# Thirteen pieces for each block of attention's tail, and an earlier place for edge features and the carried row

## The chip, the cores and the metric

The kernel runs on one core of one Trainium2 chip. The metric is device time in microseconds (us). TensorE (PE) multiplies, VectorE (DVE) and ScalarE (ACT) work element by element and read PE's results from PSUM, GpSimd (POOL) issues the gathers and SyncE (SP) issues the other DMAs. Each engine runs its own instructions in order and waits on semaphores, so a wait holds back everything written behind it on that engine.

## The reference

A graph network of 2500 nodes (width 256) and 40000 edges sorted by destination, in four layers. The change is in the code for the last two:

```python
xn = _layernorm(x, ln1_g, ln1_b)
q, k, v = heads(xn @ Wq + bq), heads(xn @ Wk + bk), heads(xn @ Wv + bv)   # 8 heads of 32
ep = ef @ We + be                                  # edge features, 64 -> 32
scores = einsum('ehd,ehd->eh', q[dst], k[src] + ep[:, None, :]) * scale * ew[:, None]
attn = softmax of scores over the edges of one dst # segment_max, exp, segment_sum
x = x + alpha * (segment_sum(attn * v[src], dst) @ Wo + bo)
x = x + beta * (gelu(layernorm(x) @ W1 + b1) @ W2 + b2)
# and then, with t = layernorm(x): top 2 of 8 experts
gate = top2(softmax(t @ router.T)); out = t
for e in range(8):
    out = out + gate[:, e] * (gelu(t @ w1[e] + b1[e]) @ w2[e] + b2[e])
```

(The projections q, k, v are made in an earlier stage, `stage_sums_experts`, and `heads` and `top2` stand for a few lines each.)

## The kernel before

`stage_attention` does all of the above except the projections. It has two kinds of work, woven into one order by `order1`.

**Edge work** runs over 79 groups of 512 edges. Group i has a slot i, with a first half (`slotA`) and a second (`slotB`). There are 86 slots, since the sums of a group come `LAG` = 7 slots after its scores. In slot i DVE adds the features to the gathered keys (`add`, L1816), multiplies by the queries in PSUM (`multiply`, L1821), reduces to scores (`reduce`, L1827) and weighs the values of group i-6 (`weigh`, L1903). PE makes the queries (`queries`, psQ, one buffer, so it waits for `product` of the group before) and features (`features`, psE) of group i+1 in `slotB`, and the sums of group i-7 (`sums`, psG) in `slotA`. ACT copies features to SBUF (`att_epb`), scales the scores and copies the sums to `part`. Every fourth slot a softmax step turns the scores (S), maxima (M) and R on PE between DVE's scans; and every fourth group a carried row goes from `part` through PE (L2209), DVE (`carry`, att_crow) and back into PE's sums (L2173).

**Block work** runs over ten blocks of 256 nodes: normalise (`att`), turn, project (`wo`), normalise, turn (`turnN`), eight feed-forward pieces (`f` up, `y` down), normalise (`norm`), turn (`turnX`), router `logits`, gates and bias (`mix`), eight experts (`A` up, `C` down), `out`. `SEGMENTS` cuts it into pieces, one for each slot. Block b starts in slot 8b+17, so below "slot 0" to "slot 7" are the eight slots from a block's start to that of the next; piece 8 of a block shares a slot with piece 0 of the next. A piece lies between the two halves of its slot on every engine. `warm` issues twelve products with zeros (L2222) ahead of the three turns. Three PSUM banks (psR) are dealt out in turn; `y` holds bank 2 while `f` uses 0 and 1.

**SP** issues per slot: the store of `part`, the load of the windows three groups ahead and the load of group i+2 (ohT, qw, eft: `load_group`, two buffers, `in_got`). In a block's slot -1, which is slot 7 of the block before, it first issues the block's three loads (L2347 to L2349) and waits until they have landed (L2375, `load`), before it goes on with the slot.

## Time and profile before

| | us |
|---|---|
| median of 3 runs (lowest, highest) | 1970.42 (1964.58, 1979.68) |
| the profiled execution, its own time | 1965.13 |
| its span, first to last instruction | 1963.7 |
| PE busy in the span | 1643.5 (84%) |
| DVE, POOL, ACT busy | 969.5, 794.7, 581.4 |
| share of full TensorE clock, mean | 0.906 |

Attention's stage begins at 949.6 us with POOL's first gather. Slots 0 to 16 have no block work; from slot 17 to the last edge slot both kinds run together; the last two blocks end alone. To read the rows: a timeline row is a start, a duration, the engine, the line, the operation, its tiles and how many instructions it merges; in square brackets stands how long the engine sat idle before it and what released it. Matmuls overlap, so their rows do too. Numbers of tiles are left out (att_t is t1 or t3, att_h is h or h1, g_mw either expert weight, g_f either feed-forward weight).

### The profile page before, as it was taken

The page shows a single profiled execution, that of the slowest core. Times are in us where ns is not written, and L with a number is a line of the kernel's source. Part 1 is how long each engine was busy: PE and PEld are TensorE (multiplying, and loading weights), DVE is VectorE, ACT ScalarE, POOL GpSimd, SP SyncE. Part 2 cuts the span into 40 slices and gives each one's busy share as a digit, 9 for nine tenths or more (in the row PEclk, how much of TensorE's full clock was granted, in tenths as well). Part 3 has the DMA queues.
Part 4 walks back from the last instruction along what each step waited for, and adds up shares of the span by engine and source line. Part 5 has one row for each costly group of instructions (what it writes and reads, how often), then busy time and mean ns, then how long its engine had stood idle before and what let it go on. Part 6 is the DMA issues. An engine that isn't in the chain of part 4 may idle for free.

```text
span 1963.7 us, 22797 instructions
## 1 busy us (share of the span) xinstructions
PE 1643.5 (84%) x6693; PEld 1054.4 (54%) x6693; DVE 969.5 (49%) x2256; ACT 581.4 (30%) x1373; POOL 794.7 (40%) x769
## 2 busy tenths in 40 slices
PE   5899579669799899996357889989998999899786
PEld 2455125235445455565233566767666767666575
DVE  5522242123332534344477677777667676674222
ACT  2111002122131222322122344343434444343322
POOL 1000564766766665000567545444445444430000
PEclk9899669779899899998566999999999999999898
DMA  7246453644645645111679755545545555531000
GB/s 241 118 166 222 138 145 81 174 135 133 179 139 144 191 129 171 31 60 59 196 219 280 209 147 148 148 138 149 159 142 150 143 160 147 150 92 34 19 6 8
DMA packets 191807, 270.02 MB, mean 138 GB/s; under 512 B 28564, under 2 KB 156273, under 8 KB 189105
## 3 DMA queue, kind: packets, MB, share of 16 engines
q1 hardware_dynamic: 147665, 144.74, 23.6%
q0 software_dynamic: 44000, 123.64, 22.7%
q8 instruction: 58, 0.95, 0.2%
q14 instruction: 84, 0.69, 0.1%
HBM read 196.22 MB, written 72.06 MB: 137 GB/s over the span
## 4 chain that ended last, share of the span: by engine, by line
PE 34%; DVE 7%; issue 4%; ACT 3%; POOL 1%; DMA 1%; SPq 1%; POOLq 0%; DVEq 0%
PE att_psR L2289 8%; PE att_psR L2316 7%; PE att_psG L2174 5%; PE att_psR L2264 4%; PE att_psR L2273 4%; POOL att_kv L1796 1%; PE att_psQ L2150 1%; PE att_psR L2250 1%; PE att_psE L2157 1%; DVE att_stat L1938 1%; PE att_psR L2308 1%; PE att_psR L2222 1%; PE att_psR L2227 1%; DVE att_n L1949 1%; PE att_psG L2173 1%
## 5 line engine op out<-in xcount | busy, mean ns | idle before, releaser
L1796 POOL DMA_INDIRECT att_kv<-table_kv,g_srcI x314 | 360.2, 1147 | 515.8 <-PE att_psG L2174 276.2
L1107 POOL DMA_INDIRECT ex_hg<-table_h,z_idx x314 | 311.3, 991 | 182.7 <-issue 86.5
L1405 PE MATMUL ex_psG<-ex_hg,ex_oh 128*42 128x256 f32 x628 | 175.6, 420 | 51.9 <-DVE ex_oh L1121 31.9
L2289 PE MATMUL att_psR<-att_t,g_mw 128*128 128x256 f32 (+1 forms) x640 | 178.1, 428 | 18.6 <-ACT att_t L2128 18.6
L2174 PE MATMUL att_psG<-att_kv,att_oh 128*42 128x264 f32 x628 | 172.3, 416 | 1.6 <-DVE att_kv L1903 0.9
L2289 PEld LDWEIGHTS att_psR<-att_t,g_mw 128*128 128x128 f32 x640 | 132.5, 215 | 46.4 <-issue 28.1
L1816 DVE TENSOR_TENSOR att_kv<-att_kv,att_epb 128x1024 f32<-128x1024 f32 x79 | 96.5, 1221 | 119.6 <-ACT att_epb L2085 82.3
L1405 PEld LDWEIGHTS ex_psG<-ex_hg,ex_oh 128*42 128x42 f32 x628 | 70.4, 126 | 155.4 <-issue 69.8
L722 PE MATMUL tab_psH<-e_u,tab_xT 128*128 128x512 f32 x320 | 146.9, 611 | 5.3 <-DVE e_u L524 5.3
L2316 PE MATMUL att_psR<-g_mw,att_h 128*128 128x256 f32 x640 | 149.2, 381 | 0.0
L2316 PEld LDWEIGHTS att_psR<-g_mw,att_h 128*128 128x128 f32 x640 | 121.8, 192 | 19.7 <-issue 3.3
L1322 ACT ACTIVATE ex_h<-ex_psH,g_cols 128x512 f32<-128x512 f32 (+2 forms) x144 | 86.0, 605 | 145.1 <-PE ex_psH L1420 123.8
L2029 DVE SCALAR_TENSOR_TENSOR att_acc<-att_psR,att_gate,att_acc 128x256 f32<-128x256 f32 x160 | 70.0, 479 | 107.2 <-PE att_psR L2316 93.3
L1433 PE MATMUL ex_psC<-e_experts,ex_h 128*128 128x256 f32 x480 | 119.2, 402 | 3.8 <-DVE ex_acc L1251 3.8
L2133 ACT ACTIVATE att_h<-att_psR,g_cols 128x256 f32<-128x256 f32 (+1 forms) x160 | 66.2, 465 | 174.6 <-PE att_psR L2289 157.2
L1420 PE MATMUL ex_psH<-ex_h,e_experts 128*128 128x512 f32 (+2 forms) x288 | 112.3, 533 | 3.3 <-ACT ex_h L1322 3.2
L2174 PEld LDWEIGHTS att_psG<-att_kv,att_oh 128*42 128x42 f32 x628 | 70.3, 125 | 82.7 <-issue 39.0
L2150 PE MATMUL att_psQ<-att_qw,att_ohT 126*128 126x256 bf16 x316 | 53.7, 297 | 70.1 <-DMA att_eft<-in_eft 33.8
L1420 PE MATMUL ex_psH<-ex_xT,e_experts 128*128 128x512 f32 (+2 forms) x288 | 111.4, 532 | 0.0
L1433 PEld LDWEIGHTS ex_psC<-e_experts,ex_h 128*128 128x128 f32 x480 | 95.0, 202 | 26.1 <-issue 12.9
L1251 DVE SCALAR_TENSOR_TENSOR ex_acc<-ex_psC,ex_gate,ex_acc 128x256 f32<-128x256 f32 x120 | 51.8, 478 | 113.1 <-PE ex_psC L1433 110.4
L722 PEld LDWEIGHTS tab_psH<-e_u,tab_xT 128*128 128x128 f32 x320 | 61.6, 195 | 78.3 <-issue 70.8
(308 smaller groups left out, 2454.4 us busy)
## 6 DMA issues: line engine op xcount, KB each, us to landing
table_h<-tab_hs SPq DMA_DIRECT2D x20, 1024.0 KB, 3.9
att_eft<-in_eft SPq DMA_DIRECT2D x158, 64.0 KB
ex_db<-table_dst SPq DMA_DIRECT2D x79, 126.0 KB
table_ohT<-ex_ohT SPq DMA_DIRECT2D x79, 126.0 KB
att_ohT<-table_ohT SPq DMA_DIRECT2D x79, 126.0 KB
table_oh<-ex_oh SPq DMA_DIRECT2D x79, 84.0 KB
att_oh<-table_oh SPq DMA_DIRECT2D x79, 84.0 KB
ex_hg<-table_h,z_idx POOLq DMA_INDIRECT x314
```

The source lines that it names most:

```text
L722: ins = nc.tensor.matmul(psH[:, c % 4, :], xT[:, b % 2, k, q * P:(q + 1) * P], Wr[:, k, j * 512:(j + 1) * 512], start=(k == 0), stop=(k == ...
L1107: nc.gpsimd.indirect_dma_start(hg[:, t % RING0, :], None, d.h[:, :], bass.IndirectOffsetOnAxis(ap=g.idx0[:, t:t + 1], axis=0)).then_inc(go ...
L1322: nc.scalar.activation((h1 if what == "A" else h2)[:, e % 2, o, 0:used(b)], psH[:, n % 3, 0:used(b)], ACT.Relu, bias=vec(g, "eb1" if what ...
L1405: ins = nc.tensor.matmul(psG[0:WG, 0:D], oh[:, i % 3, t % TP, :], hg[:, t % RING0, :], start=(t % TP == 0), stop=last)
L1420: ins = nc.tensor.matmul(psH[:, n % 3, 0:w_], w[:, e, k, o * P:(o + 1) * P], x[:, k, 0:w_], start=(k == 0), stop=(k == DK - 1))
L1433: ins = nc.tensor.matmul(psC[:, q, :], h2[:, e % 2, k, q * P:(q + 1) * P], g.w3[:, e, k, :], start=(k == 0), stop=(k == DK - 1))
L1796: nc.gpsimd.indirect_dma_start(kv[:, t % (RINGC * TP), H:H + 2 * D], None, d.kv[:, :], bass.IndirectOffsetOnAxis(ap=g.srcI[:, t:t + 1], ax ...
L1816: nc.vector.tensor_tensor(k, k, epb[:, i % 2, :, :].unsqueeze(2).to_broadcast([P, TP, H, DH]), ALU.add).then_inc(s.added, 1)
L2174: ins = nc.tensor.matmul(out[0:WG, :], oh[:, i % 3, t % TP, :], kv[:, t % (RINGC * TP), 0:H * VW], start=(t % TP == 0), stop=end)
L2264: ins = nc.tensor.matmul(out[:, 0:used(b)], g.f1[:, k, e * P:(e + 1) * P], t1[:, k, 0:used(b)], start=(k == 0), stop=(k == DK - 1))
L2289: ins = nc.tensor.matmul(out[:, c * CB:c * CB + used(b)], g.mw1[:, e, k, c * P:(c + 1) * P], t3[:, k, 0:used(b)], start=(k == 0), stop=(k ...
L2316: ins = nc.tensor.matmul(out[:, q * D:(q + 1) * D], h1[:, n % 3, k, q * P:(q + 1) * P], g.mw2[:, e, k, :], start=(k == 0), stop=(k == DK - 1))
```

## The change

The blocks are cut into thirteen pieces in place of ten, and the starts stay 8 slots apart, except that the last block may start two slots sooner (slot 87, `SLOTS + 1`). So pieces 8 to 12 of a block share slots with pieces 0 to 4 of the next. The first normalising (`att`) on DVE and the turn behind it (`turnA`) on PE are now one slot apart, `turnN` and `turnX` have slots of their own, and `logits` comes ahead of expert 0. The first turn and `turnN` lose their zero products; the output projection and `mix` get them. The features of group i+1 move from the second half of slot i to the first, behind the sums, on PE and on ACT. The turn of S comes behind the sums, the carried row ahead of the queries. The wait for the loads of a group moves from `queries` to `features`, and SP's wait for its buffer from `ep_made` to `q_ready`. The banks 0, 1, 2 are dealt out in turn, but 0 and 1 alone from a block's first `f` to its `norm`.

```diff
 SEGMENTS = (
     (("att", 0),),
+    (("turnA", 0),),
     (("wo", 0),),
-    (("turnN", 0), ("f", 0), ("f", 1), ("y", 0), ("f", 2), ("y", 1)),
-    (("f", 3), ("y", 2), ("f", 4), ("y", 3), ("f", 5), ("y", 4)),
-    (("f", 6), ("y", 5), ("f", 7), ("y", 6), ("y", 7), ("norm", 0)),
-    (("turnX", 0), ("A", 0), ("logits", 0), ("A", 1)),
-    (("mix", 0), ("A", 2), ("C", 0), ("A", 3)),
-    (("C", 1), ("A", 4), ("C", 2)),
-    (("A", 5), ("C", 3), ("A", 6), ("C", 4)),
+    (("turnN", 0),),
+    (("f", 0), ("f", 1), ("y", 0), ("f", 2), ("y", 1), ("f", 3), ("y", 2)),
+    (("f", 4), ("y", 3), ("f", 5), ("y", 4), ("f", 6), ("y", 5)),
+    (("f", 7), ("y", 6), ("y", 7), ("norm", 0)),
+    (("turnX", 0),),
+    (("logits", 0), ("A", 0), ("A", 1), ("A", 2)),
+    (("mix", 0), ("C", 0), ("A", 3), ("C", 1)),
+    (("A", 4), ("C", 2), ("A", 5)),
+    (("C", 3), ("A", 6), ("C", 4)),
     (("A", 7), ("C", 5), ("C", 6), ("C", 7), ("out", 0)))
...
-    start = [(NG // NC + 1) * (b + 1) + LAG + 2 if slots else 8 * b + 1 for b in range(NC)]
+    start = [min((NG // NC + 1) * (b + 1) + LAG + 2, SLOTS + 1) if slots else 8 * b + 1 for b in range(NC)]
...
-                elif unit == "f":
-                    n = e % 2
+                elif opened:
+                    n = turn_of = (turn_of + 1) % 3 if turn_of == 2 else (turn_of + 1) % 2
                 else:
-                    n, turn_of = turn_of, (turn_of + 1) % 3
+                    n = turn_of = (turn_of + 1) % 3
...
                         nc.scalar.copy(part[:, j % 3, :], psG[0:WG, 0:H * VW]).then_inc(s.part_ready, 1)
+                    if i + 1 < NG:
+                        features(i + 1)
...
                 def queries(i):
-                    pe.wait_ge(in_got[i % INS], 64 * (i // INS + 1))
...
                 def features(i):
+                    pe.wait_ge(in_got[i % INS], 64 * (i // INS + 1))
...
                 def slot_first(i):
                     j = i - LAG
+                    if 0 <= j < NG:
+                        sums(j)
+                    if i + 1 < NG:
+                        features(i + 1)
                     if (n := softmax(i, 0)) is not None:
...
                 def slot_second(i):
+                    j = i - LAG + 1
+                    if 0 < j < NG and j % SGG == 0:
+                        n = j // SGG
+                        pe.wait_ge(s.part_ready, j)
+                        pe.wait_ge(s.d_ready, n + 1)
+                        nc.tensor.matmul(psCarry, g.follow[0:WG, j - 1:j], part[:, (j - 1) % 3, :], start=True, stop=True).then_inc(s.carried, 1)
                     if i + 1 < NG:
                         queries(i + 1)
-                        features(i + 1)
...
                     if i >= INS:
-                        sp.wait_ge(s.ep_made, i - INS + 1)
+                        sp.wait_ge(s.q_ready, i - INS + 1)
```

How this moves instructions is seen best on PE. First the stretch behind a block's last `y` (L2273) before the change: queries, features, a turn of R, the sums, the zero products, the turn of the normalised block, then at once an expert's matmul (L2289), logits (L2296) and another expert's.

```order
L2273 MATMUL att_psR<-g_f,att_h 128x256 x4
L2150 MATMUL att_psQ<-att_qw,att_ohT 128x256 x4
L2157 MATMUL att_psE<-g_we,att_eft 128x64 x2
L2203 MATMUL att_psT<-g_ident,att_R 128x128
L2174 MATMUL att_psG<-att_kv,att_oh 42x264 x4
L2222 MATMUL att_psR<-g_none,g_identb 128x256 x12
L2227 MATMUL att_psR<-g_ident,att_n 128x128 x4
L2289 MATMUL att_psR<-att_t,g_mw 128x256 x4
L2296 MATMUL att_psR<-g_rt,att_t 128x8 x4
L2289 MATMUL att_psR<-att_t,g_mw 128x256 x4
```

The same place in the changed kernel, from the sums of slot 7 on (lines 4 to 6 higher; L2162 features, L2194 the turn of S, L2233 the turn, L2154 queries, L2300 logits):

```order
L2179 MATMUL att_psG<-att_kv,att_oh 42x264 x4
L2162 MATMUL att_psE<-g_we,att_eft 128x64 x2
L2194 MATMUL att_psT<-g_ident,att_S 128x128
L2228 MATMUL att_psR<-g_none,g_identb 128x256 x12
L2233 MATMUL att_psR<-g_ident,att_n 128x128 x4
L2154 MATMUL att_psQ<-att_qw,att_ohT 128x256 x4
L2211 MATMUL att_psT<-g_ident,att_M 1x128
L2212 MATMUL att_psT<-g_ident,att_M 1x128
L2179 MATMUL att_psG<-att_kv,att_oh 42x264 x4
L2162 MATMUL att_psE<-g_we,att_eft 128x64 x2
L2197 MATMUL att_psT<-g_ident,att_fnew 128x1
L2198 MATMUL att_psT<-g_ident,att_lnew 128x1
```

Logits and three experts' matmuls come only behind the last of these rows: the queries, two sums and two sets of features now stand between the turn's neighbours with no expert's matmul between them. The second place is the carried row (L2209) before the change, between the output projection (L2250) and `turnN`:

```order
L2250 MATMUL att_psR<-g_wo,att_t 128x256 x4
L2150 MATMUL att_psQ<-att_qw,att_ohT 128x256 x4
L2157 MATMUL att_psE<-g_we,att_eft 128x64 x2
L2209 MATMUL att_psT<-att_part,g_follow 1x264
L2174 MATMUL att_psG<-att_kv,att_oh 42x264 x3
L2173 MATMUL att_psG<-att_crow,g_ident 1x264
L2174 MATMUL att_psG<-att_kv,att_oh 42x264
L2222 MATMUL att_psR<-g_none,g_identb 128x256 x12
L2227 MATMUL att_psR<-g_ident,att_n 128x128 x4
```

And in the changed kernel (L2206 and L2178 are the carried row out and in, L2321 `C`, L2292 `A`, L2256 the output projection):

```order
L2233 MATMUL att_psR<-g_ident,att_n 128x128 x4
L2206 MATMUL att_psT<-att_part,g_follow 1x264
L2154 MATMUL att_psQ<-att_qw,att_ohT 128x256 x4
L2179 MATMUL att_psG<-att_kv,att_oh 42x264 x3
L2178 MATMUL att_psG<-att_crow,g_ident 1x264
L2179 MATMUL att_psG<-att_kv,att_oh 42x264
L2162 MATMUL att_psE<-g_we,att_eft 128x64 x2
L2292 MATMUL att_psR<-att_t,g_mw 128x256 x4
L2321 MATMUL att_psR<-g_mw,att_h 128x256 x4
L2292 MATMUL att_psR<-att_t,g_mw 128x256 x4
L2228 MATMUL att_psR<-g_none,g_identb 128x256 x12
L2256 MATMUL att_psR<-g_wo,att_t 128x256 x4
```

The queries now lie between the carried row's two products, the features behind both, and the turn, the projection and the next turn are each a slot apart with expert matmuls of the block before between them.

## Rows read from the trace of the kernel before

**Rows 1.** The page: TensorE's busy time, and its granted clock in 40 slices.
```profile
PE 1643.5 (84%) x6693; PEld 1054.4 (54%) x6693; DVE 969.5 (49%) x2256; ACT 581.4 (30%) x1373; POOL 794.7 (40%) x769
...
PEclk9899669779899899998566999999999999999898
```

**Rows 2.** The windows: stretch, its us, busy us (count) by engine, PEclk, DMA, GB/s.
```profile
1217.00:1307.00 90.00, 83.62 (x418) 62.17 (x417) 63.56 (x126) 38.00 (x101) 42.80 (x39) 0.96 0.52 150
...
1840.00:1910.00 70.00, 57.74 (x265) 47.87 (x264) 19.68 (x65) 21.15 (x38) 0.00 (x0) 0.88 0.05 16
```

**Rows 3.** The chain that ended last: each block's last `y`, blocks 0, 7, 9.
```profile
1124.40 1.74 PE att_psR L2273 x8
...
1756.37 1.74 PE att_psR L2273 x8
...
1908.13 1.74 PE att_psR L2273 x8
```

**Rows 4.** The waits, 1180 to 1720 us, PE's: total us, times, longest.
```profile
PE att_psR L2289 <- ACT att_t L2128: 12.8, 6, 2.1
...
PE att_psG L2173 <- DVE att_crow L1896: 10.1, 9, 1.6
...
PE att_psR L2264 <- ACT att_t L2118: 7.2, 6, 1.2
...
PE att_psT L2185 <- ACT att_S L2092: 5.1, 6, 0.9
...
PE att_psR L2227 <- DVE att_n L1961: 4.5, 6, 0.8
...
PE att_psR L2308 <- ACT att_gateT L2140: 3.3, 6, 0.5
```

**Rows 5.** The timeline of PE behind a block's last `y`.
```profile
1487.00 1.98 PE L2174 MATMUL att_psG<-att_kv,att_oh 128*42 128x264 f32 x8
1488.91 1.48 PE L2222 MATMUL att_psR<-g_none,g_identb 128*128 128x256 bf16 x12
...
1492.97 3.59 PE L2289 MATMUL att_psR<-att_t,g_mw 128*128 128x256 f32 x8 [2.14 <-ACT att_t L2128]
```

**Rows 6.** The timeline of SP: a store, a block's loads, the next group's load.
```profile
1505.41 0.37 SPq L2382 DMA_DIRECT2D table_o<-att_part  x1
...
1510.96 0.48 SPq L2349 DMA_DIRECT2D att_u<-table_u  x1
1518.34 0.29 SPq L2384 DMA_DIRECT2D table_o<-att_part  x1
...
1520.50 0.35 SPq L2327 DMA_DIRECT2D att_ohT<-table_ohT  x1
```

**Rows 7.** The waits of SP, 1180 to 1720 us: for the blocks' loads.
```profile
SPq L2375 <- DMA att_u<-table_u: 34.7, 6, 6.6
```

**Rows 8.** The timeline of PE, slots 17 to 19, hardly any block work.
```profile
1076.94 3.53 PE L2174 MATMUL att_psG<-att_kv,att_oh 128*42 128x264 f32 x8
...
1089.64 1.04 PE L2150 MATMUL att_psQ<-att_qw,att_ohT 126*128 126x256 bf16 x4 [3.72 <-DMA att_eft<-in_eft]
...
1099.14 1.53 PE L2174 MATMUL att_psG<-att_kv,att_oh 128*42 128x264 f32 x6
```

**Rows 9.** The timeline of SP there: the load of that group.
```profile
1085.75 0.36 SPq L2327 DMA_DIRECT2D att_ohT<-table_ohT  x1
```

**Rows 10.** The timeline of DVE behind the last `y`: `finish`, then the slot.
```profile
1486.16 0.75 DVE L1983 SCALAR_TENSOR_TENSOR att_u<-att_psR,g_rows,att_u 128x512 f32<-128x512 f32 x1
...
1490.06 1.23 DVE L1816 TENSOR_TENSOR att_kv<-att_kv,att_epb 128x1024 f32<-128x1024 f32 x1
...
1493.78 1.22 DVE L1903 TENSOR_TENSOR att_kv<-att_kv,att_p 128x1024 f32<-128x1024 f32 x1
```

**Rows 11.** The timeline of PE at the end: waits with no edge work left.
```profile
1843.87 0.66 PE L2227 MATMUL att_psR<-g_ident,att_n 128*128 128x128 f32 x4 [2.70 <-DVE att_n L1949]
...
1923.59 0.59 PE L2303 MATMUL att_psR<-g_ident,att_gate 128*8 128x128 f32 x2 [4.51 <-DVE att_gate L936]
```

More of the change, by code:

```diff
@@ L395 @@
 NCH = NREL * D // 512
+FIRST_LATER = 10
 WARM = 12
-FIRST_LATER = 10
 TABLES_FROM = NG // NB + 2
@@ L1737, in stage_attention @@
         assert redo or all(e > DONE_AFTER[b] for what, b, e in order if what == "load")
-        bank, before, last, turn_of = {}, {}, {}, 0
+        bank, before, last, turn_of, opened = {}, {}, {}, 0, False
         for what, b, e in order:
-            for unit in {"att": ("turnA",), "wo": ("wo",), "turnN": ("turnN",), "f": ("f",), "turnX": ("turnX",), "A": ("A",),
+            for unit in {"turnA": ("turnA",), "wo": ("wo",), "turnN": ("turnN",), "f": ("f",), "turnX": ("turnX",), "A": ("A",),
                          "logits": ("logits",), "mix": ("gateT", "bias"), "C": ("C",), "y": ("y",) if e == 0 else ()}.get(what, ()):
+                opened = opened or unit == "f"
                 if unit == "y":
                     n = 2
-                elif unit == "f":
-                    n = e % 2
+                elif opened:
+                    n = turn_of = (turn_of + 1) % 3 if turn_of == 2 else (turn_of + 1) % 2
                 else:
-                    n, turn_of = turn_of, (turn_of + 1) % 3
+                    n = turn_of = (turn_of + 1) % 3
                 bank[unit, b, e] = n
@@ L1752, in stage_attention @@
                 last[n] = (unit, b, e)
+            opened = opened and what != "norm"
         def drained(unit, b, e):
@@ L2107, in program @@
                                 scale(b)
-                            if b + 1 < NG:
-                                features(b + 1)
-                        if what == "att":
+                        if what == "turnA":
                             act.wait_ge(s.att_turned, b + 1)
@@ L2203, in slot_second @@
                         nc.tensor.transpose(psT[:, 0:P], R[:, :], g.ident[:, :]).then_inc(s.r_turned, 1)
-                    j = i - LAG + 1
-                    if 0 < j < NG and j % SGG == 0:
-                        n = j // SGG
-                        pe.wait_ge(s.part_ready, j)
-                        pe.wait_ge(s.d_ready, n + 1)
-                        nc.tensor.matmul(psCarry, g.follow[0:WG, j - 1:j], part[:, (j - 1) % 3, :], start=True, stop=True).then_inc(s.carried, 1)
                 def take(unit, b, e):
@@ L2232, in program @@
                         pe.wait_ge(g.loaded1, 16 * N_LOADED1)
+                        features(0)
                         queries(0)
-                        features(0)
                     for what, b, e in order:
@@ L2239, in program @@
                             slot_second(b)
-                        if what == "att":
+                        if what == "turnA":
                             out = take("turnA", b, e)
-                            warm(out)
                             pe.wait_ge(s.att_ready, b + 1)
@@ L2246, in program @@
                             out = take("wo", b, e)
+                            warm(out)
                             pe.wait_ge(s.aT_ready, b + 1)
@@ L2253, in program @@
                             out = take("turnN", b, e)
-                            warm(out)
                             pe.wait_ge(s.xn_ready, b + 1)
@@ L2300, in program @@
                             out = take("gateT", b, e)
+                            warm(out)
                             pe.wait_ge(s.gate_ready, b + 1)
```

5 lines of the change are left out of this document (1 added, 4 removed).

## The prediction, made before the changed kernel ran

> **What bounds the kernel now.** I read the page first: PE is busy for 84% of the span, and in the half that holds attention its slices show the full clock less a tenth [rows 1]. Then the windows: in 90 us of the steady part PE is busy 83.6 us, DVE 63.6, POOL 42.8, at a granted clock of 0.96 [rows 2]. Then the chain that ended last, for the pace: the last `y` of block 0 ends at 1126.1 us (1124.40 + 1.74), that of block 7 at 1758.1, that of block 9 at 1909.9 [rows 3]. So a period of eight slots takes (1758.1 - 1126.1) / 7 = 90.3 us, and 205.6 us follow from there to the end of the span. Then the waits: over six periods PE waited 43.0 us in the six rows shown, 7.2 a period, each of them short and at a fixed place: for the copy of the turned block ahead of the first expert (2.1) and ahead of the first `f` (1.2), for the carried row (1.7 in two waits), for the scores' turn (0.85), for the first turn's input (0.75) and for the gates' copy (0.55) [rows 4]. The clock costs (1 - 0.96) x 90 = 3.6 us more [rows 2]: after a wait of 2.14 us eight expert matmuls took 3.59 us where the same eight take 1.9 [rows 5]. So a period is some 79.5 us of PE's work, 7.2 of waits and 3.6 of clock. The steady part is bound by PE in order, and anything that fills its waits counts in full.
>
> **The change part by part.** No product is added or taken away on PE: three times twelve zero products before and after (1.3 us each, from 1488.91 to the turn). What moves is where PE waits.
>
> *Waits that go.* The carried row goes out ahead of the queries (0.45 us), which shortens its two waits, and expert matmuls of the block before stand between DVE's work and it: I take its 1.7 us as gone; the lower end is 2 x 0.45 = 0.9. `turnN` and the first `f` are a slot apart: 1.2 gone. First turn a slot behind `att`: 0.75 gone. The copy of the turned block ahead of the experts: 2.1 gone, since sums lie between. One of the two half-clock stretches, that behind the gates, loses the waits ahead of it: 1.8 gone. The gates' copy (0.55) stays. The scores' turn keeps its 0.85: it moves behind the sums, but in slot 3 ACT reaches the scaling only after the square root of the normalising that the projection at the end of slot 2 starts. Sum: 1.7 + 1.2 + 0.75 + 2.1 + 1.8 = 7.6 us a period.
>
> *A wait that comes.* Slots 6 and 7 are now light: PE has 2.6 us of block work (`f` 7, `y` 6, `y` 7) in one and 1.8 (zeros, turn) in the other, where it had 5 to 7. And the features of a group now come in the first half of the slot and carry the wait for the group's load, so they ask for it a whole piece of block work sooner. Take the end of the sums in slot 6 as zero. SP issues the store of that part 0.6 us later, and the last of the next block's loads 6.0 after that (1505.41 to 1511.44); it then waits 34.7 / 6 = 5.8 for their landing [rows 6, 7]; the next group's load is issued 3.3 later (1517.2 to 1520.50) [rows 6]; and from the first issue to the matmul that waits for it 3.9 us pass (1085.75 to 1089.64) [rows 8, 9]. Sum 19.6 us until the features of slot 0 can run. PE's own work up to there is: features 0.4, block 2.6, queries 0.45, sums 1.9, features 0.4, turn of S 0.2, zeros 1.3, turn 0.5, queries 0.45, turns of M 0.2, sums 1.9: 10.3 us. So PE stands still for 9.3 us in each period, where before 8 us of expert matmuls and more lay in between. Behind the waiting features stand logits and three experts, that is, everything. The same is seen in the trace where a block's load meets slots without block work: PE's sums of slot 17 start at 1076.94, and its queries wait for the load until 1089.64 [rows 8]. DVE sets a lower bound to the stall should the load be early: it holds the normalising for 3.9 us (1486.16 to 1490.06) and then four slot operations and two scans for 5.8, before it has weighed what the sums of slot 0 need [rows 10]; from the last `y` that is 9.8 us, of which PE can fill 5.4 with the work listed, so at least some 4 us of idle time stay.
>
> The net of a period is +9.3 - 7.6 = +1.7 us, over seven periods +12.
>
> *The start.* Block 0's last `y` comes in slot 23 instead of 21. Slots with little block work take 8 us (the sums of slot 17 start at 1076.94 and those of slot 19 at 1099.14, a block's load among them) [rows 8]. Work through slots 19 to 23 with the same 7.2 us from part to load, 3.6 for the normalising in slot 19 and the feed-forward pieces (13.8 us) in slots 21 to 23 gives the last `y` at some 1139 us, against 1126: +13. Slots 0 to 16 stay as they are: gathers and loads bound them; I take 0, with ends of -4 and +5.
>
> *The end.* After the last `y` of block 7 the new order has two edge slots less (5.2 us of sums and their kin, the counterpart of the +13), and in the last period queries and features run out sooner (1.7). Blocks 8 and 9 now overlap in seven pieces, not two. Of PE's waits between 1758 and 1910 us, 18.6 us, I expect 6.3 to stay: the two behind a last `y` (2.7 each) [rows 11] and short ones; 12.3 gone. The clock in 1840 to 1910 is 0.88 [rows 2], 8.4 us lost; half of the end's loss goes: 5.9. The wait of 4.5 for the gates of block 9 [rows 11] is filled by a third expert and by the zero products: 2.7 net. Sum -27.8.
>
> Total: +12 + 13 - 27.8 = -3 on a span of 1963.7 in a profiled execution of 1965.1: **1962 us**. That execution stood 5 us below the median of the runs (1970.4), so I give 1961 to 1966 as the likeliest spot and 1962 as the number.
>
> **A page beside it.** The group's load takes 3.9 us from first issue to use and the block's 5.8 after its last issue [rows 7 to 9]. The Trainium skill (DMA: Bandwidth & Descriptors, "Anatomy of one DMA") gives a fixed cost of about 2.0 us a DMA plus bytes at full rate. By it the block (three DMAs of 256 KB and more, about 0.6 us of data each) would land some 2 to 3 us sooner and the group 1 to 2, the stall would be about 5 instead of 9.3, and the total near 1932. The trace has the durations, beside gathers that run at the same time, so the sum goes by the trace.
>
> **The rivals.** *Light slots stay covered* (chance 0.22). If the loads land sooner than in the rows, or PE works on through slots 6 and 7, only DVE's bound of 4 us is left: 4 - 7.6 = -3.6 a period, -25 over seven, and 1965 - 25 + 13 - 28 = 1925. For it: the six waits that go are certain by place; the block's load need not meet a gather. Against: SP's sequence is in order and every link of it is a row.
>
> *The clock stays low* (0.23). In slots 6, 7 and 0 PE would be idle for about half of 20 us. The half clock behind a wait of only 2.14 us [rows 5] shows how little it takes, and in the first part of attention, with little block work, the page has three slices of 0.5 to 0.6 [rows 1]. If logits and the three experts' matmuls behind the stall (6.1 us at 2.4 GHz) run at 1.2 GHz throughout, and the sums of slot 0 do, that is up to 6 us where I counted 1.8, and the stall may grow with a slower landing: +4.5 a period, +31: 1993. It decides (over 1%) from about 3.4 us a period. The Trainium skill (TensorE: Matmul & The Clock Gate, "What's actually happening") says that the throttled state is the default and activity releases it; by that rule light slots cost twice, and it speaks against this change. The trace agrees as far as rows 5 go.
>
> *Nothing much moves* is the forecast itself (0.55): the waits only change place. Its own range is 1940 to 1984: two us a period either way and 5 at the start.
>
> **How the numbers follow.** About 1% (20 us) is what a measurement of this kernel can tell from no change. Faster by over 1% takes the first rival and 0.09 of the forecast: 0.31. Slower takes 0.20 of the second. The rest is 0.49. The range of 1920 to 1994 leaves out the lower half of the first rival and the upper third of the second.
>
> **What would show it.** In the changed profile: a wait of PE's features or queries for att_eft, some 5 to 9 us once a period, in the slots behind a block's loads; no wait left at the first `f`, the first turn and the experts' first matmul; the carried row's at most 0.5; a last `y` of block 0 near 1139, of block 7 near 1783, periods of 92; some 178 us from there to the end, with a clock near 0.95 in it. I am wrong if features never wait for att_eft in the steady part (then 1925 and the first rival), or if the clock in windows of slots 6 to 0 is below 0.8 and expert matmuls at 3.6 us stand in rows of more than one.

## The result, and the profile after

The changed kernel took 1993.25 us (median of nine runs, 1982.75 to 1999.89) against 1973.61 for the kernel before: a ratio of 1.0084, 95% interval 1.0059 to 1.0108. It is slower by a little under 1%, some 17 us, where I had written 1962. A second comparison on another chip (e13) gave 1.0124.

Its profiled execution took 1993.25 us with a span of 1991.6, 27.9 more than the 1963.7 before. Not all of this belongs to the change: attention's first addition on DVE (`L1821`, `L1816` before) starts at 970.07 us instead of 959.69, so 10.4 us were lost ahead of it, in stages that the change does not touch. From that addition to the end of the span it is 1021.5 against 1004.0 us: +17.5, which agrees with the ratio.

The page of the changed kernel: TensorE's busy time, its granted clock in 40 slices, and the group of the edge features (busy and mean ns of one, then idle time ahead and what ended it):

```profile
PE 1662.6 (83%) x6693; PEld 1061.9 (53%) x6693; DVE 969.5 (49%) x2256; ACT 580.5 (29%) x1371; POOL 775.3 (39%) x769
...
PEclk9899679779899899998557799898989899999998
...
L2162 PE MATMUL att_psE<-g_we,att_eft 128*128 128x64 f32 x316 | 61.3, 325 | 102.1 <-DMA att_eft<-in_eft 88.4
```

The features wait for their load, 88.4 us over the whole span. The windows, columns as in [rows 2]: from the addition of slot 24 to that of slot 72 (six periods), seventeen microseconds around slot 7 of one period, and from block 7's last `y` to the end:

```profile
1166.94:1729.25 562.31, 513.15 (x2490) 376.80 (x2490) 379.54 (x745) 229.10 (x607) 239.53 (x228) 0.94 0.50 143
...
1450.00:1467.00 17.00, 13.93 (x61) 10.36 (x62) 12.17 (x27) 4.58 (x12) 9.50 (x9) 0.70 0.70 201
...
1813.86:1991.60 177.74, 153.22 (x752) 125.61 (x752) 64.30 (x199) 55.49 (x112) 3.90 (x5) 0.94 0.06 18
```

A period is 562.31 / 6 = 93.7 us between these additions, where the same additions before were 90.4 apart. The last `y` of blocks 7 and 9 in the chain, and that of block 0 in PE's timeline, against [rows 3]:

```profile
1812.12 1.74 PE att_psR L2278 x8
...
1940.15 1.74 PE att_psR L2278 x8
```
```profile
1161.11 1.89 PE L2278 MATMUL att_psR<-g_f,att_h 128*128 128x256 f32 x8
```

Counted from attention's first addition, block 0's last `y` ends at 192.9 us (before 166.4: +26.5), block 7's at 843.8 (798.4), and 177.8 us follow (205.6: -27.8). Between the two are seven periods of 93.0 (90.3: +18.9). The three terms are the three of the forecast: +26.5 for +13, +18.9 for +12, -27.8 for -27.8.

The waits of PE, 1200 to 1760 us, against [rows 4]:

```profile
PE att_psE L2162 <- DMA att_eft<-in_eft: 35.3, 12, 4.6
PE att_psR L2313 <- ACT att_gateT L2145: 3.9, 6, 1.2
PE att_psR L2233 <- DVE att_acc L2034: 2.5, 4, 0.6
PE att_psT L2194 <- ACT att_S L2099: 1.5, 6, 0.3
```

The waits at the carried row, at the first `f` and at the experts are gone. In their place the features wait twice a period. Over exactly six periods (1166.94 to 1729.25 us) their row is 37.9 us, 6.3 a period:

```profile
PE att_psE L2162 <- DMA att_eft<-in_eft: 37.9, 12, 4.6
```

### The profile page after: what moved, and what is told of

Read it like the earlier page. It is cut to its first block, busy times and chain, and to the rows that moved or that the text cites. A ratio compares the mean times of both kernels' runs of the same rounds, so it can differ in the third digit from the quotient of the medians.

```text
span 1991.6 us, 22795 instructions
## 1 busy us (share of the span) xinstructions
PE 1662.6 (83%) x6693; PEld 1061.9 (53%) x6693; DVE 969.5 (49%) x2256; ACT 580.5 (29%) x1371; POOL 775.3 (39%) x769
## 4 chain that ended last, share of the span: by engine, by line
PE 33%; SPq 4%; issue 4%; DMA 4%; DVE 4%; POOL 1%; ACT 1%; another core or an unknown queue 0%; POOLq 0%; DVEq 0%; ACTq 0%
PE att_psR L2292 7%; PE att_psR L2321 6%; PE att_psG L2179 5%; PE att_psR L2269 3%; PE att_psR L2278 3%; DMA att_eft<-in_eft 2%; PE att_psE L2162 1%; DMA att_u<-table_u 1%; PE att_psR L2228 1%; PE att_psQ L2154 1%; POOL att_kv L1801 1%; SPq L2331 1%; SPq L2335 1%; PE att_psR L2256 1%; SPq L2333 1%
## 5 line engine op out<-in xcount | busy, mean ns | idle before, releaser
L1801 POOL DMA_INDIRECT att_kv<-table_kv,g_srcI x314 | 339.4, 1081 | 559.5 <-PE att_psG L2179 319.2
L2179 PE MATMUL att_psG<-att_kv,att_oh 128*42 128x264 f32 x628 | 175.5, 422 | 11.7 <-issue 8.6
L2292 PE MATMUL att_psR<-att_t,g_mw 128*128 128x256 f32 (+1 forms) x640 | 162.9, 408 | 0.0
L1405 PEld LDWEIGHTS ex_psG<-ex_hg,ex_oh 128*42 128x42 f32 x628 | 71.0, 127 | 161.9 <-issue 76.9
L2321 PE MATMUL att_psR<-g_mw,att_h 128*128 128x256 f32 x640 | 150.7, 384 | 0.0
L2162 PE MATMUL att_psE<-g_we,att_eft 128*128 128x64 f32 x316 | 61.3, 325 | 102.1 <-DMA att_eft<-in_eft 88.4
L2292 PEld LDWEIGHTS att_psR<-att_t,g_mw 128*128 128x128 f32 x640 | 130.4, 209 | 19.0 <-issue 0.8
L2321 PEld LDWEIGHTS att_psR<-g_mw,att_h 128*128 128x128 f32 x640 | 120.9, 191 | 19.4 <-issue 3.7
L2162 PEld LDWEIGHTS att_psE<-g_we,att_eft 128*128 128x128 f32 x316 | 49.6, 225 | 139.3 <-DMA att_eft<-in_eft 91.7
L1420 PE MATMUL ex_psH<-ex_h,e_experts 128*128 128x512 f32 (+2 forms) x288 | 112.7, 535 | 3.3 <-ACT ex_h L1322 3.2
L1433 PEld LDWEIGHTS ex_psC<-e_experts,ex_h 128*128 128x128 f32 x480 | 96.6, 205 | 27.8 <-issue 13.8
L1821 DVE TENSOR_TENSOR att_kv<-att_kv,att_epb 128x1024 f32<-128x1024 f32 x79 | 96.0, 1216 | 21.5 <-issue 8.7
```

The source lines that it names most:

```text
L1405: ins = nc.tensor.matmul(psG[0:WG, 0:D], oh[:, i % 3, t % TP, :], hg[:, t % RING0, :], start=(t % TP == 0), stop=last)
L1420: ins = nc.tensor.matmul(psH[:, n % 3, 0:w_], w[:, e, k, o * P:(o + 1) * P], x[:, k, 0:w_], start=(k == 0), stop=(k == DK - 1))
L1433: ins = nc.tensor.matmul(psC[:, q, :], h2[:, e % 2, k, q * P:(q + 1) * P], g.w3[:, e, k, :], start=(k == 0), stop=(k == DK - 1))
L1801: nc.gpsimd.indirect_dma_start(kv[:, t % (RINGC * TP), H:H + 2 * D], None, d.kv[:, :], bass.IndirectOffsetOnAxis(ap=g.srcI[:, t:t + 1], ax ...
L1821: nc.vector.tensor_tensor(k, k, epb[:, i % 2, :, :].unsqueeze(2).to_broadcast([P, TP, H, DH]), ALU.add).then_inc(s.added, 1)
L2162: ins = nc.tensor.matmul(psE[:, c * 2 * DH:(c + 1) * 2 * DH], eft[:, i % INS, c * P:(c + 1) * P], g.we[:, :], start=True, stop=True)
```

## One period, followed through

PE's timeline of one period from the end of the sums of slot 6 to slot 0 (start, us, count, then idle time ahead and its releaser):

```profile
1441.25 0.64 PE L2179 MATMUL att_psG<-att_kv,att_oh 128*42 128x264 f32 x2
...
1445.50 1.98 PE L2179 MATMUL att_psG<-att_kv,att_oh 128*42 128x264 f32 x8
1450.41 1.11 PE L2162 MATMUL att_psE<-g_we,att_eft 128*128 128x64 f32 x4 [2.94 <-DMA att_eft<-in_eft]
1451.32 0.42 PE L2194 MATMUL att_psT<-g_ident,att_S 128*128 128x128 f32 x1
1451.53 2.77 PE L2228 MATMUL att_psR<-g_none,g_identb 128*128 128x256 bf16 x12
...
1456.36 2.23 PE L2179 MATMUL att_psG<-att_kv,att_oh 128*42 128x264 f32 x8
1461.25 0.66 PE L2162 MATMUL att_psE<-g_we,att_eft 128*128 128x64 f32 x4 [2.66 <-DMA att_eft<-in_eft]
```

SP's timeline over the same stretch:

```profile
1444.06 0.34 SPq L2332 DMA_DIRECT2D att_ohT<-table_ohT  x1
...
1446.94 0.52 SPq L2352 DMA_DIRECT2D att_o<-table_o  x1
...
1448.02 0.46 SPq L2354 DMA_DIRECT2D att_u<-table_u  x1
1454.54 0.29 SPq L2389 DMA_DIRECT2D table_o<-att_part  x1
...
1456.06 0.35 SPq L2332 DMA_DIRECT2D att_ohT<-table_ohT  x1
```

A group's load is issued at 1444.06, and the block's loads follow it by 2.9 us. The features that need the group run at 1450.41, 6.3 us after the issue. SP then stands until 1454.54, 6.5 us after its last issue for the block, stores the part and issues the next group at 1456.06; the features of slot 0 run at 1461.25, 5.2 us later. The forecast put the last link 19.6 us behind the end of the sums of slot 6; those end at 1441.9 (1441.25 + 0.64), so it came at 19.4. The chain was right (a landing 1.3 us longer, the issue ahead of it 1.5 sooner). But PE was idle for only 5.6 us of it (2.94 + 2.66), not 9.3. The other part went into the work between: the twelve zero products took 2.77 us for 1.48 in [rows 5]. From the first of the two waits to the sums of slot 0 PE worked without a pause at a granted clock of 0.50, the level of 1.2 GHz:

```profile
1450.41:1456.36 5.95, 5.95 (x27) 4.43 (x27) 4.11 (x5) 1.44 (x6) 3.35 (x4) 0.50 0.86 261
```

The forecast had the same work (features, turn of S, zeros, turn, queries, turns of M) at 3.05 us; it took 5.95. The lower clock filled the hole instead of costing on top of it.

## The experiments

All times below are from the first addition of attention, so what happens ahead of it is left out. *Waits* is PE's idle time and *half clock* is (1 - granted clock) x time, both per period, over the additions of slots 24 to 72. The ratio is to the kernel before on the same chip. Ramps (slots 0 to 17) are to be compared only on one chip: the kernel before took 1972 us on chips 14 and 3 and 1936 to 1938 on chip 12. The chip of the first two rows is not on record; there it took 1973.6. Ratios rest on 4 to 10 executions of each kernel, the other columns on one profiled execution.

| kernel | chip | ratio (95%) | slot 17 | slots 9-17 | period | waits | half clock | block 0's `y` | end |
|---|---|---|---|---|---|---|---|---|---|
| before | | 1 | 118.7 | 58.6 | 90.4 | 7.2 | 3.4 | 166.4 | 205.6 |
| changed | | 1.008 (1.006-1.011) | 130.2 | 64.1 | 93.7 | 8.2 | 5.4 | 192.9 | 177.8 |
| e1 | 14 | 0.982 (0.979-0.985) | 119.5 | 56.1 | 88.0 | 6.0 | 2.3 | 179.3 | 176.3 |
| e2 | 14 | 0.983 (0.980-0.986) | 113.4 | 56.6 | 87.9 | 5.8 | 1.4 | 177.2 | 177.6 |
| e3 | 14 | 0.994 (0.991-0.997) | 128.0 | 64.1 | 89.6 | 5.7 | 3.4 | 188.0 | 177.5 |
| e4 | 14 | 1.029 (1.024-1.034) | 122.0 | 60.5 | 97.8 | 10.1 | 7.1 | 175.6 | 211.2 |
| e5 | 12 | 1.010 (1.005-1.014) | 112.7 | 62.8 | 93.8 | 8.5 | 5.4 | 177.0 | 175.8 |
| e6 | 12 | 0.995 (0.992-0.998) | 108.9 | 57.5 | 92.0 | 7.6 | 4.9 | 164.4 | 177.3 |
| e7 | 12 | 0.979 (0.974-0.984) | 107.7 | 57.4 | 88.1 | 6.1 | 2.3 | 162.0 | 177.8 |
| e8 | 12 | 0.999 (0.997-1.002) | 106.8 | 54.7 | 90.4 | 7.2 | 3.4 | 152.3 | 207.6 |
| e9 | 12 | 0.984 (0.980-0.988) | 112.0 | 60.6 | 88.0 | 6.2 | 2.3 | 175.5 | 176.6 |
| e10 | 12 | 1.016 (1.011-1.021) | 119.4 | 65.3 | 92.5 | 7.1 | 4.8 | 168.3 | 206.0 |
| e11 | 12 | 0.982 (0.978-0.986) | 107.6 | 57.2 | 87.8 | 6.0 | 2.0 | 166.5 | 175.8 |
| e12 | 12 | 0.988 (0.984-0.991) | 108.3 | 57.4 | 90.7 | 7.3 | 3.7 | 161.9 | 177.4 |
| e13 | 3 | 1.012 (1.010-1.015) | 133.3 | 67.2 | 94.9 | 8.9 | 6.3 | 198.8 | 176.2 |
| e14 | 3 | 1.009 (1.006-1.012) | 122.1 | 62.0 | 94.9 | 8.9 | 6.3 | 187.2 | 179.6 |
| e15 | 3 | 0.977 (0.976-0.979) | 122.9 | 58.7 | 87.6 | 5.7 | 1.1 | 181.7 | 176.3 |

In every row the period less its waits and its half clock is 79.5 to 80.8 us. This is PE's work, and the two other columns say where each period goes.

**The load, undone in three ways.** e1 puts the features back behind the queries:

```diff
                 def queries(i):
+                    pe.wait_ge(in_got[i % INS], 64 * (i // INS + 1))
...
                 def features(i):
-                    pe.wait_ge(in_got[i % INS], 64 * (i // INS + 1))
...
                 def slot_first(i):
...
-                    if i + 1 < NG:
-                        features(i + 1)
...
                 def slot_second(i):
...
                         queries(i + 1)
+                        features(i + 1)
```

with ACT's copy behind the scaling and SP's wait on `ep_made` as before.

> The changed kernel with one part undone: the products of the edge features (and ACT's copy of them, and the wait for a group's load, which SP again answers to) stand behind the queries in the second half of a slot, as before the change. Thirteen pieces, the carried row and the scores' turn stay as changed. Theory L (the features now ask for a group's load a piece of block work sooner, and PE stands still for it in the light slots and in the ramp ahead of the first block): the features' waits of 5.6 to 7.3 us a period and those of the ramp (+11 us from slot 0 to slot 17) go. Steady period near 89 us instead of 93, slot 17 some 10 us sooner after slot 0, total 1993 - 28 - 10 = 1955, ratio to the kernel before 0.985 to 0.995. Rival P (the period is set by DVE or by the clock in the light slots that the thirteen pieces leave, whatever waits there): the wait moves to the queries with the same length, period 92 to 93, total within 5 us of the changed kernel, ratio 1.005 to 1.011. Rival N (the ramp's 11 us are the luck of one execution): ramp unchanged.

e2 adds a third buffer:

```diff
-INS = 2
+INS = 3
...
-                        load_group(0, features)
-                        load_group(1, features)
+                        for i in range(INS):
+                            load_group(i, features)
```

> The changed kernel with three buffers instead of two for a group's inputs (one-hot rows, queries, edge features): each group is loaded one slot sooner, nothing else moves. Theory L: a load is then there a slot (8 to 11 us) before it is wanted, so every wait of the features for their load goes, in the period (5.6 to 7.3 us) and in the ramp: total near 1993 - 30 to - 40 = 1955 to 1963, ratio 0.985 to 0.993. Rival P (DVE or the clock sets the light slots): the features wait less but the sums or queries wait for DVE instead; period 91 to 93, ratio 1.00 to 1.01.

e3 takes the wait for the block's loads out of SP's queue:

```diff
                             load_block(b)
-                            if not redo:
-                                sp.wait_ge(blk_got[b % 2], 48 * (b // 2 + 1))
```

> The changed kernel without the wait in SP's queue for the landing of a block's own loads (DVE waits for them itself where it uses them). So SP goes on 5.8 us sooner to the store of the part and to the next group's load, once in a period. Theory S (the stall in the light slots is made by this link of SP's order, as my sum had it: 5.8 of its 19.6 us): the features' longer wait of each period shrinks by its whole length (2.9 us) and part of the second, total near 1993 - 20 = 1973, ratio 0.995 to 1.002; the ramp stays as it is. Rival G (the group's load is late of itself, by its landing and by the moment at which it is asked for): no change, ratio 1.006 to 1.011.

e1 and e2 agree: with the features late, or early with a buffer more, the loss of 0.8% becomes a gain of 1.8%, the period falls by 5.7 and 5.8 us, and slot 17 comes 11 and 17 us sooner. Both medians are a little better than theory L said. PE's waits over six periods of e1, with no row for the load left:

```profile
PE att_psR L2312 <- ACT att_gateT L2145: 8.8, 6, 2.2
PE att_psG L2179 <- issue: 7.9, 6, 1.3
PE att_psT L2192 <- ACT att_S L2097: 7.6, 11, 1.0
PE att_psQ L2155 <- DVE att_kv L1826: 5.6, 6, 0.9
```

Without the first row 4.5 us a period are left, with the first turn's 0.8, near my lower bound of 4. The queries and the first turn wait for DVE and the scores' turn for ACT's scaling of DVE's scores. For the sums' 7.9 us the profile names no releaser; DVE's weighing of their values ends 0.1 us ahead of their start in all six. e3 takes away half:

```profile
PE att_psE L2162 <- DMA att_eft<-in_eft: 18.1, 10, 3.1
```

The features' 6.3 us a period become 3.0, and the half clock falls by 2.0 with them; the ramp, where one block only is loaded, keeps its 64.1 us in slots 9 to 17. So SP's blocked queue is one half of the stall, a load that is late of itself the other. The ratio of 0.994 is just below theory S's 0.995.

**The parts alone.** e4 is the kernel before with only the features moved (the edit of e1 the other way round). e10 moves the carried row ahead of the queries and the scores' turn behind sums and features as well:

```diff
                 def slot_second(i):
+                    j = i - LAG + 1
+                    if 0 < j < NG and j % SGG == 0:
...
+                        nc.tensor.matmul(psCarry, g.follow[0:WG, j - 1:j], part[:, (j - 1) % 3, :], start=True, stop=True).then_inc(s.carried, 1)
                     if i + 1 < NG:
                         queries(i + 1)
```

> The kernel before with one part of the change done alone: features, their copy on ACT and the wait for a group's load in the first half of a slot, SP asking for the next load as soon as the queries are made. Block pieces, carried row and scores' turn stay as before. Theory L: the ramp (slots 0 to 17) gets 8 to 11 us longer, and in the period the load is asked for a piece of block work sooner but the slots are heavy, so 0 to 3 us a period: ratio 1.004 to 1.015. Rival P (pieces and their light slots cause all of it): ratio 0.996 to 1.002, ramp unchanged.

> The kernel before with the moves inside a slot alone: features early, carried row ahead of the queries, scores' turn behind sums and features; the block's work stays in nine pieces. It is the counterpart of e6, and e4 with the carried row and the turn moved too. In e4 (features early alone) the waits grew by 2.9 us a period (1.6 of it at the carried row, since the features no longer stand between it and the sums) and the half-clock stretches by 3.7. Theory F (the features were the cover of the carried row): with the row ahead of the queries its 3.3 us of waits go and the clock comes back in part, period 92 to 94.5 instead of 97.8, ratio 1.005 to 1.02. Rival L (it is the load, asked for a piece sooner): period 96 to 98, ratio 1.025 to 1.03.

Theory L failed at e4. The kernel is 2.9% slower, for 0.4 to 1.5% expected: the period grew by 7.4 us, not by 0 to 3, with little waiting for the load, and slot 17 comes 3 us later than in the first row, not 8 to 11. PE's waits over six periods of e4, and of e10:

```profile
PE att_psG L2173 <- DVE att_crow L1896: 19.9, 12, 2.0
...
PE att_psE L2157 <- DMA att_eft<-in_eft: 4.3, 8, 1.8
```
```profile
PE att_psG L2173 <- DVE att_crow L1896: 9.0, 7, 1.9
...
PE att_psE L2157 <- DMA att_eft<-in_eft: 5.6, 5, 1.9
```

In e4 the carried row's wait doubles from 10.1 us [rows 4] to 19.9: the features' 0.5 us had been the cover between the queries and the sums. In e10 it is 9.0, the half clock falls from 7.1 to 4.8, and the period from 97.8 to 92.5. Theory F's range holds, though its "gone" does not: half of the wait stays. Nor is all of this the row's: e10 moves the scores' turn too, and its wait, 7.5 us over e4's six periods, is gone as well. So of the 3.0 us of waits saved a period 1.8 are at the carried row and 1.2 at the turn, and the half clock's 2.3 can't be divided between them. The load's own waits in e10 are 0.9 us a period by the second row; how much of the half clock hangs on it was not tried.

e6 is the other half: pieces, zero products, bank rotation and the last start as changed, all moves undone. e9 is e6 with the scores' turn behind the sums:

```diff
                 def slot_first(i):
+                    if 0 <= j < NG:
+                        sums(j)
                     if (n := softmax(i, 0)) is not None:
...
-                    if 0 <= j < NG:
-                        sums(j)
```

> The kernel before with the thirteen pieces alone (with what belongs to them: the first turn a piece of its own, zero products at the output projection and ahead of the gates' turn, the wait for the turned block at the logits, the bank rotation, the last block's start two slots sooner). Features, carried row and scores' turn stand where they stood before. Theory A (the gain lies in the pieces, at the first turn, first f and first expert 4.1 us of waits a period, and in the end): period 88.5 to 89.5 instead of 90.4, end 25 us shorter, total 1936 to 1952, ratio 0.982 to 0.990. Rival C (the carried row's place is what makes the difference, since its 1.7 us a period come back as 3 behind light slots): period above 90, ratio 0.990 to 0.996.

> The kernel of e6 (thirteen pieces, features late) with the turn of the scores behind the sums, as the change has it; the carried row stays at the end of the slot. It splits the 4.0 us a period that lie between e6 (92.0) and e1 (88.0). Theory T (the turn of the scores is what counts: in e6 PE waits 5.25 us a period for it, in front of sums that are ready): period 88.0 to 89.3, ratio 0.980 to 0.986. Rival C (the carried row is what counts): period 91 to 92, ratio 0.990 to 0.996.

PE's first row of waits over six periods, e6 and then e9:

```profile
PE att_psT L2190 <- ACT att_S L2097: 34.4, 13, 2.9
```
```profile
PE att_psT L2192 <- ACT att_S L2097: 9.6, 13, 1.0
```

The pieces alone make the period longer (92.0 for 90.4): the waits of [rows 4] at the carried row, the first `f` and the experts go, but in a light slot the scores' turn stands ahead of sums that are ready and waits 5.3 us a period for ACT (twelve waits; the row holds a thirteenth at the window's edge). Behind the sums it waits 1.4, and the period is 88.0. So behind thirteen pieces the turn's place is worth 4.0 us, and the carried row's nothing: e9 has it late, e1 early, both take 88.0. Theory A of e6 failed by the period, and its rival was right in number but blamed the wrong instruction.

**Zero products and start.** Both on e7, which has the three edits of e1 to e3 at once.

> The changed kernel with the features late again, a third buffer for a group's inputs and no wait in SP's queue for a block's loads, all three at once. If the load was one cause with three handles (theory L), the handles don't add up: either of the first two alone gave 0.982, and together they give 0.976 to 0.983, with the ramp at 112 to 115 us and a period near 87.5. If they are separate costs, they add: 0.970 or less.

> The kernel of e7 with the twelve zero products ahead of the first turn and of the second turn (n1), as before the change, instead of ahead of the output projection and of the gates' turn. Theory Z (where they stand sets only which wait they fill, and little work follows a turn in the light slots): period within 0.5 us of 88.1 and the end 2 to 3 longer, since the wait for block 9's gates is bare again; ratio 0.979 to 0.983. Rival K (they keep the clock up for the experts behind the gates): the period grows by 1.5 us or more, ratio above 0.985.

> The kernel of e7 (features late, third buffer, no wait for a block's loads in SP's queue) with the last block's start two slots later, at 89, as it was before. My sum put the end at 178 us from block 7's last y instead of 205.6, with the two slots less as 5.2 of it and the rest as waits and clock at the seam of blocks 8 and 9. If so the end grows from 177.8 by 5 to 12 us, ratio 0.981 to 0.986. Rival: the start is the whole of the 28 us: end near 200, ratio above 0.99.

e12's edit against e7 (e11's takes the `min` out of `start`):

```diff
                             out = take("turnA", b, e)
+                            warm(out)
...
                             out = take("wo", b, e)
-                            warm(out)
...
                             out = take("turnN", b, e)
+                            warm(out)
...
                             out = take("gateT", b, e)
-                            warm(out)
```

e7 is one cause with three handles: 0.979, no better than e1 or e2 by their intervals. In e12 the same 36 zero products a period, elsewhere, cost 2.6 us a period (90.7 for 88.1), 1.3 of it waits and 1.4 half clock. Theory K's numbers hold, its cause by half: the half clock rose, but as much of the loss is the gates' wait laid bare, which is theory Z's. The end, which I had 2 to 3 us longer, did not move (177.4 for 177.8), since two things cancel: its waits and half clock rose by 2.2 us, but only seven sets of zero products lie in it, for eight in e7. The waits over six periods of e12, and of e7:

```profile
PE att_psR L2312 <- ACT att_gateT L2145: 16.3, 6, 3.2
```
```profile
PE att_psR L2312 <- ACT att_gateT L2145: 9.0, 6, 2.2
```

e11 was a miss for both theories: the end is 175.8 us, not 183 to 190. The last start is worth nothing; e6 and e10 (177.3 and 206.0) show that the pieces make the whole of the end.

**The ramp.** e5 and e14 are one kernel, the changed one with the scores' turn ahead of the features; e5 ran on a chip where the changed kernel did not, so it told only the period: 93.8, unchanged, where theory Q had up to 1 us less. Its ratio of 1.010 lies in the rival's range, its slot 17 at 112.7 in neither's.

```diff
                         sums(j)
-                    if i + 1 < NG:
-                        features(i + 1)
                     if (n := softmax(i, 0)) is not None:
...
+                    if i + 1 < NG:
+                        features(i + 1)
```

> The changed kernel with the turn of the scores put ahead of the features (behind the sums, as the change has it), so that in every fourth slot it no longer stands behind their wait for the load. Theory Q (half of what the early features cost is that the softmax's first step is queued behind their wait, which matters in the ramp, where slots have no block work): slot 17 comes 4 to 9 us sooner after slot 0 (121 to 126 instead of 130), the steady period falls by up to 1 us (93.7 to 92.7), total ratio 1.000 to 1.006. Rival L (the wait for the load itself is the cost, whatever stands behind it): ramp and period within 1 us of the changed kernel, ratio 1.006 to 1.011.

> The changed kernel as it is, for the ramp on the same chip as e14 and e15. Theory Q (the turn of the scores queued behind the features' wait is over half of the ramp's loss): slot 17 comes 116 to 121 us after slot 0 and 5 us or more later than in e14. Rival L (the wait alone): within 2 us of e14. In both the period is 93.7 and the ratio 1.006 to 1.013.

> The kernel of e5 (scores' turn ahead of the features), on the same chip as e13. Theory Q: slot 17 at 110 to 114 us after slot 0, ratio 0.003 to 0.005 lower than e13's. Rival L: ramp and ratio as e13.

> The changed kernel with the features early as changed, a third buffer for a group's inputs, and no wait for a block's loads in SP's queue: e7 but for the place of the features. With no load to wait for, the features' place in the slot should not matter: ramp at 106 to 109 us, period 87.7 to 88.2, ratio 0.977 to 0.983, that is e7's 0.979. If the early features cost something of their own (in ACT's order, say), the ramp is above 111 or the period above 89, ratio above 0.985.

> The kernel before with three buffers instead of two for a group's inputs, nothing else. In the steady part it has no wait for the load, in the ramp 16.5 us in six waits of the queries. Theory L: the steady period stays at 90.4 (within 0.3), the ramp and the first block's load slots get 5 to 10 us shorter, ratio 0.994 to 0.998. Rival: the load's waits in the ramp only move to the gathers and to DVE behind them: ratio 0.999 to 1.001.

On one chip slot 17 comes at 133.3 us with the turn behind the features and at 122.1 with it ahead, and block 0's last `y` at 198.8 and 187.2; the periods are equal. By this difference of 11 us theory Q holds; its absolute numbers, taken from another chip, were 8 to 17 us too low, and the intervals of the two ratios (1.012 and 1.009) overlap a little. How it comes about is seen in the changed kernel, slot 8, in the ramp, PE's timeline:

```profile
1023.91 1.98 PE L2179 MATMUL att_psG<-att_kv,att_oh 128*42 128x264 f32 x8
1029.80 0.72 PE L2162 MATMUL att_psE<-g_we,att_eft 128*128 128x64 f32 x4 [3.91 <-DMA att_eft<-in_eft]
1030.31 0.42 PE L2194 MATMUL att_psT<-g_ident,att_S 128*128 128x128 f32 x1
```

and DVE's:

```profile
1023.95 1.23 DVE L1821 TENSOR_TENSOR att_kv<-att_kv,att_epb 128x1024 f32<-128x1024 f32 x1 [0.49 <-ACT att_epb L2092]
1030.77 0.42 DVE L1839 TENSOR_TENSOR_SCAN att_fwd<-att_mk,att_psT 128x128 f32<-128x128 bf16 x1 [5.60 <-PE att_psT L2194]
```

PE has nothing to do for 3.9 us, the turn stands behind that wait, and DVE, whose scan comes ahead of its product in program order, stands for 5.6. So a load that is late for PE stops DVE too, once in four slots. All the traces bear this out: from slot 0 to slot 17 DVE idles ahead of that scan for 13.5 to 15.7 us in the changed kernel, e3 and e10, and for 28.4 in e13 (one wait of 12.7 among them that the profile puts down to another load). These four have the turn behind features that wait. In the other thirteen traces it is at most 3.8. Slots 9 to 17, which leave out the first, irregular ones, take 55 to 59 us with the features late or a third buffer and 60.5 to 62.8 with the features early and the turn ahead; 64 to 67 with the turn behind them. e9's 60.6 falls out of this, so some 3 us here are the luck of one execution. On chip 3 the turn's place is 5.2 of slots 9 to 17 (67.2 for 62.0) and the late load itself 3.3 (62.0 for e15's 58.7), but over the whole ramp e14 and e15 are equal (122.1 and 122.9), so those 3.3 are not shown. Chip 12 gives the same order: e10, with the turn behind early features, reaches slot 17 at 119.4, e5, with the turn ahead, at 112.7, and the six kernels with late features at 106.8 to 112.0. The turn's place is the larger part on both.

e15 is e7 with the features early, and takes a ratio of 0.977 and a period of 87.6 for e7's 0.979 and 88.1: where the load is not late, the early features cost nothing in the period. For the ramp this is open: its 122.9 missed the 106 to 109 that I had taken from another chip, and no kernel with late features ran on chip 3. e8 shows that the third buffer does nothing for the kernel before (0.999, where theory L had at most 0.998 and a shorter ramp). e15 and e7 beat both kernels.

## Why the prediction was wrong

**The start, +13 forecast and +26.5 measured.** The step that failed is the sentence "Slots 0 to 16 stay as they are: gathers and loads bound them; I take 0, with ends of -4 and +5". From slot 17 to block 0's last `y` it took 62.7 us for 47.7, +15.0, close to the 13. In slots 0 to 17 it took 11.5 us more. I had weighed the features' earlier wait in the light slots of the period and not in the slots that are lightest of all, and had not asked what is queued behind it on PE (the scores' turn) and who waits for that (DVE). e13 and e14 show this (133.3 and 122.1 us to slot 17), e1 and e2 that it starts with the load.

**The period, +1.7 forecast and +2.7 to +3.3 measured.** The term that failed here is the clock's, which had the wrong sign. *Waits that go*, forecast 5.8 without the clock, are measured so: carried row 1.7, first `f` 1.15 and experts 2.1 gone as said; the first turn kept 0.6 of its 0.75, and the scores' turn lost 0.6 where I had it keep all; 5.7 in sum. *The wait that comes* has the length that the chain gave (19.4 for 19.6), but 6.3 us of idle time for 9.3. *The clock* was to give back 1.8 and took 2.0: 5.4 us at half clock a period for 3.4 [rows 2 has 0.96, the window above 0.94]. So stall and clock together are 11.7 us (6.3 + 5.4), where I had 11.1 (9.3 + 1.8). The chain and the sign of the net were right, its parts were not. What I did not see is that the scores' turn and the places of the zero products move a period by 4.0 and 2.6 us; I had costed them at nothing. The carried row's place, for which I had 1.7, made no difference between e9 and e1.

**The end, -27.8 forecast and -27.8 measured**, the parts less well: PE's idle time fell from 40.4 to 24.5 us, 15.9 for the 15 that I had (12.3 + 2.7); the half clock from 20.2 to 11.3, 8.9 for 5.9; and the work that is left gave 3.0 for 6.9. That the sum met is luck. e11 shows that the two slots of the last start gave nothing.

**The rivals.** *The clock stays low* had 1993 and the measurement 1993.25, but that is a meeting of numbers: it put +4.5 on a period and +13 at the start. By the first half of the mark that I had set it was right: the clock from 1446 to 1470 us is 0.79 and from 1450 to 1467 0.70. By the other half it was not, for it wanted logits and three experts at 1.2 GHz throughout. The row of these 24 expert matmuls is

```profile
1463.29 7.11 PE L2292 MATMUL att_psR<-att_t,g_mw 128*128 128x256 f32 x24
```

and only seven of them ran at the full length of the lower clock, 0.63 us each for 0.38. Per period it was 8.5 expert matmuls, against 13 in the kernel before, so the half clock moved from the experts to the light slots ahead of them. The Trainium skill (TensorE: Matmul & The Clock Gate, "What's actually happening") has it that the throttled state is the default and activity releases it; the trace agrees, with 0.50 behind a wait of 2.94 us and 0.98 from 1466 to 1490 us, where PE was busy for 23.46 of 24. *Light slots stay covered* is what e2 and e15 show once the load is out of the way: 2.5 and 2.8 us a period less than before, where that rival had 3.6. The fixed cost of about 2.0 us that the Trainium skill gives for a DMA (DMA: Bandwidth & Descriptors, "Anatomy of one DMA", which is about DMAs that GpSimd issues, while these are SyncE's) would have led to it. The trace does not agree: the load took 6.3 and 5.2 us from its first issue to the features.

What stays open: why e4 loses 3.7 us a period to the clock on 2.9 us of waits, and how much of a ramp is luck. Slots 0 to 9 alone take 50 to 54 us on chip 12 and 57 to 66 elsewhere.

## What to carry to other kernels

When a wait for a transfer is moved forward in an engine's order, price it first in the slots with the least work, and list what is queued behind it and who waits for that. An instruction that looks free may be the cover of another wait (the features for the carried row, the zero products for the gates), so a move is costed at both of its places. And where PE sets the pace, write its time as work + waits + (1 - clock) x time: work stayed within 1% of its middle in 17 traces of 15 kernels, and nearly all of every difference was in the other two.

## What the runs showed of the hardware

The clock and the waits go together but not in proportion: from e2 to e4 the waits rose from 5.8 to 10.1 us a period and the half clock from 1.4 to 7.1. Two sets of twelve zero products, 1.5 us each, are worth 2.6 us a period by their place alone. Chips differ ahead of the steady part and in the ramp, where PE and DVE wait for loads and gathers, and not in the period of the kernel before, where PE sets the pace. That kernel took 1936 to 1938 us on chip 12 and 1972 on chips 14 and 3, while the period of e8 on chip 12 is its 90.4 again; e8's attention began at 940.9 us for 959.7, and its slot 17 came at 106.8 for 118.7.
